# Attention's unit of 64 score pairs cut into five stretches instead of eight

## What is computed

```python
q, k, v = heads(x @ Wq + bq), heads(x @ Wk + bk), heads(x @ Wv + bv)   # 16 heads of 32
scores = jnp.einsum('bhqd,bhkd->bhqk', q, k) / np.sqrt(HD)             # 2048 x 2048 per head
attn = jax.nn.softmax(scores, axis=-1)
out = jnp.einsum('bhqk,bhkd->bhqd', attn, v)
```

## Time and profile before

| | us |
|---|---|
| median of three runs | 3128.03 (3121.56 to 3131.3) |
| profiled execution, its time | 3132.72 |
| its span, first to last instruction | 3131.3 |
| attention in it, first pair to last values | about 351 to 1887 |

### The profile page before, as it was taken

How to read it: one execution, slowest core, us unless ns; L and a number is a source line. 1 busy time by engine, 2 the same in 40 slices (tenths; PEclk the granted TensorE clock), 3 DMA queues, 4 the chain that set the end, 5 groups by cost and what they waited for, 6 DMA issues and landing times.

```text
span 3131.3 us, 42990 instructions
## 1 busy us (share of the span) xinstructions
PE 3076.8 (98%) x16138; PEld 2144.6 (68%) x16138; DVE 2156.5 (69%) x3633; ACT 1388.4 (44%) x2703; POOL 1542.9 (49%) x655
## 2 busy tenths in 40 slices
PE   8999999999999999999999999899999999999999
PEld 7887655555555555555555546688888888778998
DVE  4457889998999999989999976443333333237776
ACT  2221466666666666666666672221111111013333
POOL 0000389889888898898898973200000000102222
PEclk9999999999999999999999999999999999899999
DMA  6674687879779788797887776520111110212221
GB/s 206 187 228 150 175 169 169 193 150 198 167 165 201 151 189 174 167 199 150 181 182 160 164 155 230 187 81 6 35 41 41 41 41 29 98 59 68 78 82 61
DMA packets 169366, 423.39 MB, mean 135 GB/s; under 512 B 18493, under 2 KB 60605, under 8 KB 141864
## 3 DMA queue, kind: packets, MB, share of 16 engines
q0 software_dynamic: 27744, 201.08, 31.7%
q1 hardware_dynamic: 139639, 214.07, 22.8%
q10 hardware_dynamic: 1776, 5.51, 0.7%
HBM read 143.51 MB, written 75.50 MB: 70 GB/s over the span
## 4 chain that ended last, share of the span: by engine, by line
PE 94%; DVE 2%; DMA 2%; issue 1%; POOL 1%; ACT 1%; SPq 0%; DVEq 0%; ACTq 0%; POOLq 0%
PE ps L384 16%; PE ps L672 15%; PE ps L683 15%; PE ps L1194 12%; PE ps L1181 11%; PE ps L460 5%; PE ps L1728 4%; PE ps L464 3%; PE ps L1745 3%; PE ps L689 2%; PE ps L1766 1%; PE ps L1045 1%; PE ps L1531 1%; PE ps L158 1%; PE ps L293 1%
## 5 line engine op out<-in xcount | busy, mean ns | idle before, releaser
L397 DVE TENSOR_REDUCE nmp<-ps 128x1 f32<-128x512 f32 x1966 | 1200.0, 681 | 108.2 <-PE ps L384 103.9
L762 ACT ACTIVATE pt<-ps 128x512 f32<-128x512 f32 x2048 | 1031.0, 625 | 458.7 <-PE ps L672 455.5
L861 POOL TENSOR_TENSOR pt<-pt 128x2048 f32<-128x2048 f32 x217 | 995.9, 4589 | 119.6 <-ACT pt L762 113.3
L672 PE MATMUL ps<-qs,ks 128*128 128x512 f32 x2048 | 810.6, 400 | 2.5 <-ACT pt L762 2.5
L384 PE MATMUL ps<-ks,qs 96*128 96x512 f32 x1966 | 803.5, 409 | 0.1
L384 PEld LDWEIGHTS ps<-ks,qs 96*128 96x128 f32 x1966 | 372.6, 190 | 265.3 <-DVE nmp L397 167.8
L683 PE MATMUL ps<-pt,vq 128*32 128x512 f32 x4096 | 493.6, 599 | 0.0
L672 PEld LDWEIGHTS ps<-qs,ks 128*128 128x128 f32 x2048 | 389.4, 191 | 96.2 <-ACT pt L762 19.5
L1181 PE MATMUL ps<-hpb,w 128*128 128x512 f32 x1536 | 382.6, 399 | 3.4 <-DMA x_d<-x 3.4
L1194 PE MATMUL ps<-w,gp 128*128 128x512 f32 x1536 | 380.5, 396 | 3.1 <-DVE gp L1305 3.1
L1303 DVE CAST gp<-g 128x512 fp32r<-128x512 f32 x128 | 61.7, 482 | 403.7 <-ACT g L1292 403.7
(11 more groups left out here) (169 smaller groups left out, 2874.9 us busy)
## 6 DMA issues: line engine op xcount, KB each, us to landing
pt<-pt POOLq DMA_DIRECT2D x189, 1024.0 KB, 8.7
qk_d<-st SPq DMA_DIRECT2D x128, 256.0 KB, 2.9
qs<-qk_d SPq DMA_DIRECT2D x87, 256.0 KB, 5.0
ks<-qk_d SPq DMA_DIRECT2D x42, 512.0 KB, 8.5
xina<-in_x SPq DMA_DIRECT2D x8, 1024.0 KB, 6.4
v_d<-vst SPq DMA_DIRECT2D x32, 256.0 KB, 3.1
vq<-v_d SPq DMA_DIRECT2D x32, 256.0 KB, 4.3
ao_d<-accs SPq DMA_DIRECT2D x32, 256.0 KB, 7.1
```

Of the source, the lines that this page charges most:

```text
L397: dve.tensor_reduce(nmp[:, n // 4, n % 4:n % 4 + 1], ps[:, ring.bank["max", u], :], AX.X, ALU.max, negate=True).then_inc(s_mr, 1)
L672: pe.matmul(ps[:, score_bank(n), :], ksb[w % 2][:, hh, 128 * kt:128 * kt + 128], qsb[:, v % 3, hh, :], start=True, stop=True).then_inc(s_s ...
L762: act.activation(pt[:, exp_slot(g), hh, :], ps[:, score_bank(n), :], ACT.Exp, scale=SCALE).then_inc(s_exp, 1)
L861: pool.tensor_tensor(accumulator(v, 0), accumulator(v, 0), pt[:, exp_slot(g), :, :], ALU.add).then_inc(s_add, 1)
```

## The change

For units 0 to 30 the eight phases of 8 pairs with 2 key tiles of values behind each become stretches of 13, 13, 13, 13 and 12 pairs, with the values of key tiles 14 and 15 of the unit before, then 0 to 4, 5 to 7, 8 to 10 and 11 to 13 behind them. The sums of the unit before stand behind pair 26 (before: pair 24), the row ahead of pair 50 (counted from 0; before: 48). All four parts of the reciprocals stand together on VectorE behind maximum 26, ahead of the sums' copy. ScalarE copies the finished values after exp 13 (before: 8). The last unit keeps phases of eight. POOL and SP are not touched.

```diff
+BLOCKS = {13: (-2, -1), 26: (0, 1, 2, 3, 4), 39: (5, 6, 7), 52: (8, 9, 10), 64: (11, 12, 13)}
+SUMS_AT, ROW_AT = 26, 50
...
-            for p in range(NGRP // 2):
-                v, f = divmod(p, 8)
-                if f == 6 and v + 1 < NU:
-                    pe_row(v + 1)
+            for v in range(NU - 1):
+                for i in range(64):
+                    if i == ROW_AT:
+                        pe_row(v + 1)
+                    if EARLY - 2 + 64 * v + i < 64 * NU:
+                        pe_max(EARLY - 2 + 64 * v + i)
+                    pe_scores(16 * v + i // 4, i % 4)
+                    for kt in BLOCKS.get(i + 1, ()):
+                        if 16 * v + kt >= 0:
+                            pe_values(16 * v + kt)
+                    if i + 1 == SUMS_AT and v:
+                        pe_sums(v - 1)
+            for f in range(8):
+                g = 16 * (NU - 1) + 2 * f
                 for i in range(8):
-                    u = EARLY - 2 + 8 * p + i
-                    if u < 64 * NU:
-                        pe_max(u)
-                    pe_scores(2 * p + i // 4, i % 4)
-                if p:
-                    pe_values(2 * p - 2)
-                    pe_values(2 * p - 1)
-                if f == 2 and v:
-                    pe_sums(v - 1)
+                    pe_scores(g + i // 4, i % 4)
+                pe_values(g - 2)
+                pe_values(g - 1)
+                if f == 2:
+                    pe_sums(NU - 2)
...
+            for v in range(NU - 1):
+                for i in range(64):
+                    if i == ROW_AT:
+                        dve_row_split(v + 1, ring.bank["row", v + 1])
+                    u = EARLY - 2 + 64 * v + i
                     if u < 64 * NU:
                         dve_max(u)
                         if u % 64 == 63:
                             dve_row_max(u // 64)
-                if v >= 2 and f < 3:
-                    dve_recip(v - 2, ((0,), (1,), (2, 3))[f])
+                    if i + 1 == SUMS_AT:
+                        if v >= 2:
+                            dve_recip(v - 2)
+                        if v:
+                            dve_sums(v - 1)
```

More of the change, by code:

```diff
@@ L96, in __init__ @@
         self.uses = []
-        for p in range(NGRP // 2):
-            v, f = divmod(p, 8)
-            if f == 6 and v + 1 < NU:
[L100 to L103, removed]
-            if f == 2 and v:
-                self.use(("sums", v - 1))
+        for v in range(NU - 1):
+            for i in range(64):
+                if i == ROW_AT:
+                    self.use(("row", v + 1))
+                if EARLY - 2 + 64 * v + i < 64 * NU:
+                    self.use(("max", EARLY - 2 + 64 * v + i))
+                if i + 1 == SUMS_AT and v:
+                    self.use(("sums", v - 1))
+        self.use(("sums", NU - 2))
         self.use(("sums", NU - 1))
@@ L714, in pe_attention @@
             pe.wait_ge(s_vev, 4 * NC8 - 3)
-            for p in range(NGRP // 2):
-                v, f = divmod(p, 8)
-                if f == 6 and v + 1 < NU:
-                    pe_row(v + 1)
-                for i in range(8):
-                    u = EARLY - 2 + 8 * p + i
-                    if u < 64 * NU:
-                        pe_max(u)
-                    pe_scores(2 * p + i // 4, i % 4)
-                if p:
-                    pe_values(2 * p - 2)
-                    pe_values(2 * p - 1)
-                if f == 2 and v:
-                    pe_sums(v - 1)
+            for v in range(NU - 1):
+                for i in range(64):
+                    if i == ROW_AT:
+                        pe_row(v + 1)
+                    if EARLY - 2 + 64 * v + i < 64 * NU:
+                        pe_max(EARLY - 2 + 64 * v + i)
[3 more added lines that the diff above has]
+                            pe_values(16 * v + kt)
+                    if i + 1 == SUMS_AT and v:
+                        pe_sums(v - 1)
+            for f in range(8):
+                g = 16 * (NU - 1) + 2 * f
+                for i in range(8):
+                    pe_scores(g + i // 4, i % 4)
[3 more added lines that the diff above has]
+                    pe_sums(NU - 2)
             pe_out_tile(0)
@@ L770, in act_attention @@
         def act_attention():
[L771 to L777, removed]
+            for v in range(NU - 1):
+                for i in range(64):
+                    act_exp(16 * v + i // 4, i % 4)
+                    if i + 1 == 13 and v:
+                        act_values(v - 1)
+            for f in range(8):
+                for i in range(8):
+                    act_exp(16 * (NU - 1) + 2 * f + i // 4, i % 4)
+                if f == 0:
+                    act_values(NU - 2)
+                if f in (4, 5):
                     act_out_turn(f - 4)
@@ L822, in dve_attention @@
                             dve_row_max(u // 64)
-                if v >= 2 and f < 3:
-                    dve_recip(v - 2, ((0,), (1,), (2, 3))[f])
-                if f == 3 and v == NU - 1:
-                    dve_recip(v - 1)
[L827 to L832, removed]
+                    if i + 1 == SUMS_AT:
[3 more added lines that the diff above has]
+                            dve_sums(v - 1)
+            v = NU - 1
+            for f in range(8):
+                if f in (0, 2):
+                    dve_split_wo(f)
+                    dve_split_wo(f + 1)
+                if f == 1:
+                    dve_recip(v - 2)
+                if f == 3:
+                    dve_sums(v - 1)
+                    dve_recip(v - 1)
+                for kt in (2 * f, 2 * f + 1):
+                    if kt in LAST_DVE:
+                        dve_add(kt)
+                if f in (5, 6):
+                    dve_out_turn(f - 5)
         def pool_values(v):
```

## The result

The changed kernel takes 3196.36 us in the median of four runs (3194.99 to 3201.34), before 3127.06 in the same comparison (3121.56 to 3131.3). The ratio is 1.0226 with a 95% interval of 1.0205 to 1.0246: 2.3% slower, 69 us. Forecast were 3200.6 us and 72.6 us more.

What follows compares the result with a forecast made beforehand. TensorE, 98% busy, bounds the kernel, VectorE second. Per ordinary unit, 3.44 us of new waiting less 0.97 gained and 0.08 lost anyway gives +2.39; with units 0 and 30, +72.6 on 3128.0 gives 3200.6 us, range 3168 to 3224.

Steps and rivals of the forecast that it cites:

- The blocks' price: TensorE's values: each block costs 0.32 us for entering and leaving its form; three fewer save 0.97 us per unit.
- The stretches: Runs of pairs on TensorE: waits for VectorE's reductions add 3.44 us per ordinary unit, net +2.39.
- Unit 0: First unit, 26 pairs in one stretch: loses 2.17 us there, +2.5 us net in all.
- The row's stretch: Pairs 39 to 51: 0.48 us plus 0.37 for the row maximum and 0.60 for the row's bank, 1.45 in sum.
- Reciprocals at nothing: VectorE ahead of the sums' copy: four grouped reciprocals, 3.5 us, hidden behind five tiles and the sums; 0 added.
- Exp 36 not late: ScalarE's exp of key tile 9 waits for POOL's first accumulating DMA; up to 12.5 us costs TensorE nothing.
- a second wait on top: Rival: accumulating DMAs over 12.5 us delay exp 36, or the row's transpose costs a switch; 3211 to 3231, chance 0.12.
- The rule beside it: VectorE's PSUM reduction at 0.658 us instead of 0.597: change costs about 75 us more, 3275; chance 0.01.
- The faster rival: Only the blocks count and VectorE's waits vanish: 3098 us if fully hidden, chance 0.04.

Runs made afterwards that it cites:

- run 3: The changed kernel with VectorE's reductions of maxima over 384 of the 512 columns: 3114.28 us, ratio 0.9941 to the kernel before.
- run 2: The changed kernel with the row ahead of pair 52, right behind the block, instead of pair 50: 3189.17 us, ratio 1.0179.
- run 1: The changed kernel with eight stretches of 8 pairs again, sums at 24, row at 48, reciprocals still grouped: 3157.63 us, ratio 1.0082.
- run 7: The kernel before, order untouched, with three banks instead of four for maxima, row and sums: 3237.45 us, ratio 1.0341.

## Why the prediction was right, point by point

- **The blocks' price** (0.32 us each, 0.97 per unit) holds: 3.37 us from score to score for three tiles, 6.81 for five and the sums (6.8 was forecast), and units of 47.17 in run 3 where nothing else came between, which is 48.11 less 0.97 but 0.03.
- **The stretches.** Over units 2 to 27, the five take 6.06, 6.06, 6.26, 7.04 and 5.47 us from first to last score, where 0.467 per pair gives 5.60 four times and 5.14. So they lose 0.46, 0.46, 0.66, 1.44 and 0.33; forecast were 0.48, 0.48, 0.68, 1.45 and 0.35. A unit takes 50.37 us in the mean of units 1 to 29, before 48.14: 2.22 more, forecast 2.39, so the forecast is 5 us too high over 29 units. Unit 0 took 2.4 more (forecast 2.5), unit 30 1.1 more (0.7): behind pair 45 it has no maxima, its scores follow ScalarE's exps at 0.49, and the forecast left that out. In sum attention took 68.0 us more in the two profiled executions, for 72.6 forecast, and this is the 4 us by which 3200.6 is too high.
- **Unit 0** was right in part by luck. Its first 26 pairs lost 2.16 us, forecast 2.17. But in its row's stretch it is not VectorE that comes first: exp 44 waits 1.00 us for the accumulating DMA of key tile 5, score 47 comes 1.38 us behind score 46, and VectorE catches up meanwhile. The stretch loses 1.40 all the same, where 1.45 was forecast.
- **The row's stretch**, the least sure term, was right in both parts: run 2 takes away the 0.60 and leaves the 0.37.
- **Reciprocals at nothing** holds because of their cover, and run 1 shows the price with two tiles and the sums as cover: 0.9 us per unit.
- **Exp 36 not late** was right, and easily: POOL's chain now starts when the last unit's DMAs have landed, and the first DMA of unit 14 took 7.7 us instead of 9.8. But I watched the wrong exps. The chain of accumulating DMAs is tighter further on: exp 60 needs key tile 9, and there it came 0.53 us late once in the changed kernel (unit 28 took 50.62) and often in run 3, besides exp 44 of unit 0. The rival "a second wait on top" had the right mechanism in the wrong place. That it shows so little in the changed kernel fits with units that VectorE's waits had made 2.2 us longer: without them, in run 3, such waits are eight instead of two.
- **The rule beside it.** The 0.658 us that the Trainium skill (VectorE: DVE Perf Modes, "The TRN2 errata") gives for a read of 512 elements from PSUM is not the pace here either: the reductions of the change stand 0.598 apart, as before. **The faster rival** needed a reduction under 0.54 us; run 3 gave it 0.47, and the time moved towards its 3098: 3114 and, without the DMA, 3107.

## What to carry to other kernels

When a fast producer and a slow consumer meet over n banks, the consumer's average share says little: the stretch that the producer runs without a pause must be no longer than the banks allow. Here that is 4 banks x 0.60, less the 1.22 us from the start of a maximum to the end of its reduction, over a difference of 0.13 per pair: 9 pairs, and 4.4 with three banks, where run 7 shows a first wait at the fifth weight load. Without the 1.22 one would reckon with 18 pairs, and be wrong. Lengthening a stretch saves its fixed switch once and pays the difference for each further pair, so write down the line of both engines before choosing a length, with everything else that stands in the consumer's queue or takes a bank on the way. And read distances between starts, not busy shares: the waits here were for the most part booked as busy matmuls.

## What the runs showed that was not expected

- POOL's records grew without its pace changing. The page of the changed kernel, its additions and its DMAs:

```profile
L877 POOL TENSOR_TENSOR pt<-pt 128x2048 f32<-128x2048 f32 x217 | 1112.4, 5126 | 4.9 <-ACT pt L770 0.3
...
L869 POOL DMA_DIRECT2D pt<-pt x189 | 261.2, 1382 | 225.9 <-PE ps L685 214.7
```

Before, an addition was 4.58 us and an issue 0.88. POOL's timeline of the changed kernel shows records that overlap:

```profile
1036.28 5.31 POOL L877 TENSOR_TENSOR pt<-pt 128x2048 f32<-128x2048 f32 x1
1040.80 1.65 POOL L869 DMA_DIRECT2D pt<-pt  x1
1041.74 5.34 POOL L877 TENSOR_TENSOR pt<-pt 128x2048 f32<-128x2048 f32 x1
```

From addition to addition are 5.46 us, the 4.58 and 0.88 of before. With work always waiting, a record begins before the one ahead of it has ended; POOL had become no slower.

- Such a wait hardly shows in TensorE's own list: in the changed kernel it has 6.9 us for the maxima and 9.8 for the row's transpose, and the loss was 69. The list of the weight loads has 208.8 us behind VectorE's reductions, but 167.8 in the kernel before, where they cost next to nothing: neither list gives the price.
